# Pairs of edges spread over counting, ranking and scatter, and 12 instead of 16 of them beside every 16 state slots

## What is computed

```
xn = layernorm(x)                                   # no weights
proj = xn @ gat_w.T  (4 heads of 64);  s_src, s_tgt = per-head scores
e = leaky_relu(s_src[src] + s_tgt[tgt], 0.2);  exp_e = exp(e - max(e))
agg = segment_sum(proj[src] * exp_e, tgt) / segment_sum(exp_e, tgt)
h_local = layernorm(elu(agg + xn + gat_b))
deg = count of edges by src;  perm = argsort(deg + noise);  inv = argsort(perm)
y = mamba(xn[perm])      # conv of 4, then h = exp(dt*A) * h + dt*x*B, 16 states; y = h . C + D*x, gated
h_attn = layernorm(xn + y[inv]);  gate, feed-forward, layernorm;  x2 = x + that
out = x2 + sum of the 2 chosen of 8 experts of layernorm(x2)
```

## Time and profile before

| | |
|---|---|
| median of 3 runs | 4287.28 us (4280.2 to 4293.75) |
| profiled execution | 4285.63 us, span 4284.0 us, mean granted clock 0.839 |
| TensorE matmuls, weight loads | 3021.3 us (71%), 2270.9 us (53%) |
| VectorE | 3010.5 us (70%) |
| ScalarE | 1979.5 us (46%) |
| GpSimd | 2331.1 us (54%) |
| read from and written to memory | 389.97 MB and 63.43 MB |

### The profile page before, as it was taken

How to read it: one execution, slowest core, us unless ns; L and a number is a source line. 1 busy time by engine, 2 the same in 40 slices (tenths; PEclk the granted TensorE clock), 3 DMA queues, 4 the chain that set the end, 5 groups by cost and what they waited for, 6 DMA issues and landing times. The chain is left out here.

```text
span 4284.0 us, 66432 instructions
## 1 busy us (share of the span) xinstructions
PE 3021.3 (71%) x17205; PEld 2270.9 (53%) x17206; DVE 3010.5 (70%) x5576; ACT 1979.5 (46%) x4255; POOL 2331.1 (54%) x2215
## 2 busy tenths in 40 slices
PE   5333321177887888778887788787877488939998
PEld 4333311155655565556655565555655245528887
DVE  6677795478788878888788888888887488721111
ACT  2000000066666656666666666666665265613222
POOL 2000003557777777777777777777775357633443
PEclk8555555589998999999999999999998799969999
DMA  3100201334444444445444444444447433326665
GB/s 100 34 0 0 100 1 41 106 96 132 125 124 128 131 127 125 130 129 133 125 126 130 129 128 129 125 127 132 126 128 103 115 73 96 89 95 144 142 144 108
DMA packets 282877, 457.71 MB, mean 107 GB/s; under 512 B 56232, under 2 KB 202905, under 8 KB 282265
## 3 DMA queue, kind: packets, MB, share of 16 engines
q0 software_dynamic: 119472, 287.74, 28.4%
q1 hardware_dynamic: 163048, 165.86, 13.1%
HBM read 389.97 MB, written 63.43 MB: 106 GB/s over the span
## 5 line engine op out<-in xcount | busy, mean ns | idle before, releaser
L679 POOL DMA_INDIRECT el_g<-table,el_ix x1792 | 1796.5, 1003 | 689.7 <-issue 520.6
L1094 PE MATMUL fl_ps<-el_g,el_oh 128*128 128x260 f32 x3584 | 1029.4, 438 | 336.0 <-DVE ACC L802 333.0
L1094 PEld LDWEIGHTS fl_ps<-el_g,el_oh 128*128 128x128 f32 x3584 | 747.6, 215 | 707.5 <-issue 554.5
L822 DVE TENSOR_TENSOR_SCAN mb_h<-mb_dA,mb_h,mb_dB 128x224 f32<-128x224 f32 x896 | 573.9, 672 | 0.0
L792 DVE TENSOR_TENSOR el_g<-el_g,fl_pw 128x1024 f32<-128x1024 f32 x448 | 544.2, 1215 | 0.0
L953 ACT CAST el_oh<-fl_pt 128x512 f32<-128x512 bf16 x451 | 261.0, 579 | 425.0 <-PE fl_pt L1070 421.7
L1117 PE MATMUL fl_py<-mb_hc,ident 128*128 128x448 f32 x896 | 422.2, 553 | 0.1
L968 ACT ACTIVATE mb_dA<-mb_dt,mb_a 128x224 f32<-128x224 f32 x900 | 382.6, 475 | 2.9 <-DVE mb_dt L866 1.6
L811 DVE TENSOR_TENSOR mb_dB<-mb_u,fl_pbc 128x448 f32<-128x448 f32 x449 | 276.3, 615 | 135.4 <-PE fl_pbc L1107 134.5
L468 POOL DMA_INDIRECT sorted_x<-XN,rank x49 | 47.8, 975 | 588.8 <-DVEq L388 574.2
L939 ACT ACTIVATE el_away<-el_dst,el_less 128x512 bf16<-128x512 bf16 x452 | 325.3, 720 | 22.1 <-DVE mb_a L756 21.2
(11 more groups left out here) (300 smaller groups left out, 5405.8 us busy)
## 6 DMA issues: line engine op xcount, KB each, us to landing
el_dst<-dst_rows SPq DMA_DIRECT2D x452, 128.0 KB
el_g<-table,el_ix POOLq DMA_INDIRECT x1792
ex_w<-in_moe_W SPq DMA_DIRECT2D x56, 512.0 KB
ex_x<-routed_x SPq DMA_DIRECT2D x56, 257.0 KB, 2.8
mb_x<-sorted_x SPq DMA_DIRECT2D x30, 224.0 KB, 3.2
table<-px_tr POOLq DMA_DIRECT2D x49, 130.0 KB, 2.3
px_x<-in_x SPq DMA_DIRECT2D x49, 128.0 KB, 2.6
xn<-XN SPq DMA_DIRECT2D x1, 6272.0 KB
```

What stands on the lines that cost most here:

```text
L679: pool.indirect_dma_start(out=G[b // GU][:, b % GU * NJ + j, :], out_offset=None, in_=dram["table"], in_offset=bass.IndirectOffsetOnAxis(a ...
L822: nc.vector.tensor_tensor_scan(H[:, n % 2, k, :], dA[:, n % 4, k, :], dB[:, n % 2, k, :], H0[:, k, n % NS:n % NS + 1], ALU.mult, ALU.add). ...
L1094: mm = nc.tensor.matmul(pS, OH[:, n % (2 * GU), j, :], G[n // GU % 2][:, n % GU * NJ + j, :], start=j == 0, stop=j == NJ - 1)
```

## The change

`degrees`, `ranks` and `both_loops` become one stage, `streams`, of three blocks with barriers of all engines between them but no clearing of the edge semaphores. Pairs and state slots are numbered apart. There are 440 pairs.

1. `project`: no XN in SBUF. GpSimd's queue stores XS to `xn` in memory, tile by tile, ahead of the table rows of the same seven tiles; VectorE waits for that store before it writes XS again.
2. `pair_tables` comes straight after `project`.
3. Counting block, pairs 0 to 35. 34 steps of 46 edges instead of 46 of 34; the one-hots are laid out [value, edge], compared with REP, the values repeated 46 times, so that the innermost run of every operand is the 46 edges. TensorE reads weights and moving columns with a step of 46 elements.
4. Ranking block, pairs 36 to 91. Tiles are compared in the order 0, 48, 1, 47 and so on, one in each slot from the sixth on.
5. Third block. Pairs 92 to 95: after each one's gathers GpSimd issues 13 of the row scatters, from nine buffers that SyncE refills from `xn`. SyncE waits for all of them and loads the first block; pairs 96 to 103 go beside the preparing of block 0, two pieces each. Then 448 state slots, with pairs beside slots 0, 1 and 2 of every 4: 12 beside 16. GpSimd runs its own loop over 24 pairs in each turn, 5 ahead.

The inner functions of the edges and of the state (`logits`, `scale`, `add`, `one_hot`, `gather_sums`, `scan`, `prepare` and the others) are as before. Unchanged too: `nodes`, `plan`, `experts`.

```diff
-DB = 34
+DB = 46
+ND = DC // DB                      # 1564 // 46 = 34
+GB = 24
+G_COUNT, G_RANK, G_INTRO, G_LEAD = 36, 92, 104, 5
+PAIRS = G_INTRO + NC // 2 * GB      # 104 + 14 * 24 = 440
+def pair_beside(m):
+    at = m.n % 4
+    return Slot(m.i, G_INTRO + m.n // 4 * 3 + at, GB) if at < 3 else None
 # project, VectorE
-    nc.vector.tensor_scalar(at, X[:, j, :], ...)          # XN
     dve.wait_ge(turned, 1 + i * TG)
+    dve.wait_ge(kept_xn[j], 16 + i * 16)
     nc.vector.tensor_scalar(XS[:, j, :], X[:, j, :], ...)
 # project, GpSimd
+    for j in range(TG):
+        pool.wait_ge(scaled, 1 + i * TG + j + 1)
+        pool.dma_start(n_t[...], XS[:, j, :]).then_inc(kept_xn[j], 16)
+        def edges_vector(dve, S):
+            steps = logits(dve, S) if S.n % GU == 0 else None
...
+            add(dve, S - 3)
...
+            scale(dve, S - 1)
+        def edges_tensor(pe, S):
+            turn(pe, S + (GU - 1))
+            spread(pe, S + (GU - 1))
+            gather_sums(pe, S - 2)
 # counting block, VectorE
+    def mark_high(c):
+        if c >= 2:
+            dve.wait_ge(counted, c - 1)
+        nc.vector.tensor_tensor(HA[:, c % 2], HI[:, c * DB:(c + 1) * DB].unsqueeze(1).to_broadcast([P, SRC_HI, DB]),
+                                REP[:], ALU.is_equal).then_inc(split_hot, 1)
+    for q in range(G_COUNT):        # logits' first step before mark_high
+        mark_high(q); ...; add(dve, S - 3); ...; scale(dve, S - 1); mark_low(q)
 # counting block, TensorE
+    for q in range(G_COUNT):
+        edges_tensor(pe, pair(q))
+        c = q - 1
+        pe.wait_ge(split_hot, 2 * c + 2)
+        for e in range(DB):
+            mm = nc.tensor.matmul(count[:], HA[:, c % 2, :, e], HB[:, c % 2, :, e], ...)
+        mm.then_inc(counted, 1)
 # ranking block
+    tile_at = [t for u in range(NT // 2) for t in (u, NT - 1 - u)] + [NT // 2]
+    for q in range(G_COUNT, G_RANK):
+        edges_vector(dve, pair(q))
+        if first <= q < first + NT:
+            compare(q - first)
 # third block, GpSimd
+    for k in range(SCAT + PREP):    # 4 + 8
+        p = pair(G_RANK + G_LEAD + k)
+        free(pool, p)
+        gather(pool, p, srcT[:, p.number, :])
+        for t in range(k * each, min((k + 1) * each, NT)):
+            pool.wait_ge(xn_loaded[b], t // len(XN) * 16 + 16)
+            pool.indirect_dma_start(out=dram["sorted_x"], in_=XN[b], ...).then_inc(placed[b], 16)
 # third block, SyncE
+    for k in range(SCAT):
+        for t in range(ahead + k * each, min(ahead + (k + 1) * each, NT)):
+            bring(t)                # waits placed[b] of tile t - 9
+        rows(sp, pair(G_RANK + k + 4))
+    for b in range(len(XN)):
+        sp.wait_ge(placed[b], -(-(NT - b) // len(XN)) * 16)
+    load(0)
+    for k in range(SCAT, SCAT + PREP):
+        rows(sp, pair(G_RANK + k + 4))
 # the slot of the loop, VectorE (ScalarE, TensorE and SyncE alike)
-    def slot(S, last=False):
+    def slot(M, S):                 # S is pair_beside(M), None in every fourth slot
...
+        if S:
+            add(dve, S - 3)
...
+        if S:
+            scale(dve, S - 1)
         prepare(c + 1, 1 - b, at)
-        inflow(S + 1)
+        inflow(M + 1)
```

More of the change, by code:

```diff
@@ L154, in build @@
         stage(constants)
[L155 to L159, removed]
+        stage(project, a, dram)
         with nc.sbuf_tensor("ACC", [P, NT, ROW], F32) as ACC, nc.sbuf_tensor("emax", [P, NH], F32) as emax, \
@@ L201, in project @@
     passed = sem("passed")
+    kept_xn = [sem(f"xn_stored{j}") for j in range(TG)]
     wv, wv_sb, eps_set, kept = sem("score_weights"), sem("score_weights_sb"), sem("eps_set1"), sem("score_kept")
@@ L608, in both_loops @@
     brought = [sem(f"fl_dst{g}") for g in range(4)]
+    early = lambda v, least: isinstance(v, int) and v < least
     with ExitStack() as ctx:
@@ new lines, in free, with gather @@
+        def free(pool, p):
+            if not early(p.number, 2 * GU):
+                pool.wait_ge(s["summed"], p.number - 2 * GU + 1)
+                apart(pool, s["passed"])
+        def gather(pool, p, index):
+            b = p.n % (2 * GU)
+            for j in range(NJ):
+                pool.indirect_dma_start(
+                    out=G[b // GU][:, b % GU * NJ + j, :], out_offset=None, in_=dram["table"],
+                    in_offset=bass.IndirectOffsetOnAxis(ap=index[:, j:j + 1], axis=0)).then_inc(gathered[b], 16)
@@ new lines, in turn, with spread @@
+        def turn(pe, p):
+            q, n = p.number, p.n
+            pe.wait_ge(s["hot"], q + 1)
+            if not early(q, 1):
+                pe.wait_ge(s["turned_sb"], q)
+            for j in range(NJ):
+                mm = nc.tensor.transpose(pT[:, j, :], OHT[:, n % 2, j * P:(j + 1) * P], I16[:])
+            mm.then_inc(s["turned"], 1)
+        def spread(pe, p):
+            q, n = p.number, p.n
+            pe.wait_ge(s["hot"], q + 1)
+            if n % GU == 0 and not early(q, GU):
+                pe.wait_ge(s["logit"], p.of(GU) * 5)
+            k = pe.value_load(tile_of[0:1, bass.ds(q, 1)], min_val=0, max_val=NT - 1)
+            for j in range(NJ):
+                mm = nc.tensor.matmul(pX[:, n % GU * NJ + j, :], OHT[:, n % 2, j * P:(j + 1) * P],
+                                      parts[:, bass.ds(k, 1), :].rearrange("p o c -> p (o c)"),
+                                      start=True, stop=True, skip_group_check=True)
+            mm.then_inc(s["spread"], 1)
@@ new lines, in gather_sums @@
+        def gather_sums(pe, p):
+            q, n = p.number, p.n
+            pe.wait_ge(s["scaled"], q + 1)
+            pe.wait_ge(s["turned_sb"], q + 1)
+            if not early(q, 1):
+                pe.wait_ge(s["added"], q)
+            for j in range(NJ):
+                mm = nc.tensor.matmul(pS, OH[:, n % (2 * GU), j, :], G[n // GU % 2][:, n % GU * NJ + j, :],
+                                      start=j == 0, stop=j == NJ - 1)
+            mm.then_inc(s["summed"], 1)
+        def edges_vector(dve, S):
+            steps = logits(dve, S) if S.n % GU == 0 else None
+            if steps:
+                next(steps)
+                next(steps)
+                next(steps)
+            add(dve, S - 3)
+            if steps:
+                next(steps)
+                next(steps)
+            scale(dve, S - 1)
```

1332 lines of the change are left out of this document (686 added, 646 removed).

## The result

The changed kernel takes 4364.51 us (median; 4363.57 to 4365.64) against 4284.25 for the kernel before on the same chip: ratio 1.0184, 95% interval 1.0168 to 1.02. It is slower by 1.8%; I had forecast 4085. Its profiled execution took 4363.7 us, with a span of 4362.1.

The account below looks back on a forecast made before the run. GpSimd's queue was taken to bound the loop, full for 94% of the period, VectorE next. Span 4284.0 + 122 (front) - 323 (loop) = 4083, given as 4085 us; range 3985 to 4185.

Parts of the forecast that it names:

- 46 count matmuls are 4.1 at 1.2: Counting block, TensorE: the count matmuls of one slot take 4.1 us at 1.2 GHz, 2.05 if they scale with the clock.
- the ring: Counting slot: add, gather_sums, count matmuls, mark_high wait on each other in turn; 7.6 us at full clock, 11.3 at half, 8.9 taken.
- the phase: Counting block of 36 slots, 34 with marks at 8.9 us each: 339 us in all.
- The loop: State loop: a period of 16 slots falls from 87.45 to 75.9 us, giving 323 us less.
- the one for the B/C copies: State loop: VectorE's wait for copies that stand behind the convolution on TensorE stays at about 4.8 us a period.
- rival (c): State loop: TensorE takes over, the gather wait becomes one for TensorE; period 80, 113 us more, 4198; chance 10 in 100.
- Marks at 0.58 ns an element: Counting block, VectorE: with adjacent 16-bit elements mark_high takes 2.6 us and mark_low 1.7.
- rival (a): Counting block: marks stay at 1.09 ns an element, mark_high 4.9 us; 85 us more, 4170; chance 12 in 100.
- rival (b): Ranking block: comparisons hold GpSimd's gathers, 3.8 us for two slots, 93 in all, 4178; chance 8 in 100.
- Ranking: Ranking block: 49 slots with a comparison at 6.0 us, 7 at 5.2 and 3 for the barrier, 333 us.
- Rival (d): State loop: engine hand-overs keep slots without a pair at 3.67 us; period 85.7, kernel 4357, slower; chance 4 in 100.
- 122 us later: Everything ahead of the state loop: first state slot at 995 us instead of 873, from 176 + 339 + 333 + 147.

Follow-up runs that it names:

- the fastest kernel: Changed kernel with each mark value stored adjacently, the addition before mark_high and each mark written in two halves of 23 edges: 4048.8 us, ratio 0.9451 to the kernel before.

## Why the prediction was wrong

**The step that failed**: "46 count matmuls are 4.1 at 1.2 (89 ns each, 139.8 / 1564, where the granted clock was 0.50) and 2.05 if they scale". The 89 ns are those of a matmul whose operands lie adjacent. I had noted that the layout was turned and priced that for VectorE alone, which writes the marks; for TensorE, which reads them, I took the row of the old layout, and gave the link no upper bound. Measured: 8.44 us at either clock level. It enters the ring with 4.4 us over the value at half clock and 6.2 over that at full clock; it also keeps TensorE busy, and the granted clock was 0.56 there against 0.71 with adjacent reads, so gather_sums was 3.5 to 3.8 us in every slot, near its half-clock value. Ring 14.95 instead of 8.9, 34 x 6.05 = 206 of the 225 us by which the phase was missed; the kernels with adjacent reads give 194 back, directly.

**The other 19 us of that phase** lie all but one ahead of the first mark: 38 us from the start of the phase (178) to mark_high instead of 20. VectorE waited there 19.1 us for the first gathers, of which the first was held for 16.37 us. In the kernels without REP it is not held and the first mark comes 13.7 us sooner; what holds it stays open.

**Point by point.**
- Projection and pair tables: 178 for 176. The loop: 77.0 for 75.9, on VectorE's work of 64.9 us a period (1816.12 / 28), as said, but the idle time stands elsewhere. The wait for gathers is gone, as said; the one for the B/C copies, which I kept at 4.8, fell to 0.5 a period; in its place VectorE waits for the logits' inputs from TensorE. Two groups of the loop from 1500 to 3300 us, 23.4 periods:

```profile
L1020 DVE TENSOR_TENSOR mb_dB<-mb_u,fl_pbc 128x448 f32<-128x448 f32 x371 | 226.6, 611 | 12.8 <-PE fl_pbc L1258 12.0
...
L516 DVE TENSOR_REDUCE el_s<-fl_px 128x128 f32<-128x384 f32 x70 | 38.9, 555 | 193.8 <-PE fl_px L604 172.1 <-issue 21.8
```

- 172.1 / 23.4 = 7.4 us a period: the wait for TensorE of rival (c) did come. It took the place of other idle time, so the period is 1.1 us over the forecast and not the 4.1 at which (c) was priced. That the period came out near 75.9 is in part luck: the idle time was kept at 10.7 us for one reason and is 12.1 for another.
- Marks at 0.58 ns an element: 2504 and 1683 ns for 2.6 and 1.7, rival (a) refuted. The row that the 0.58 came from is an int32 shift with one input, so no row bore it out for two bf16 inputs. By the Trainium skill (VectorE: DVE Perf Modes, the perf-mode tier table), where a bf16 tensor_tensor in SBUF has twice the plain rate, mark_high is an estimated 2.5 us; the trace agrees.
- Comparisons hold no gather: beside them (780 to 1090 us) a gather takes 950 ns; rival (b) refuted. Marks hold them: 1670 ns in the mean with the ring opened. The Trainium skill (SBUF — State Buffer, SBUF: two separate sides) says that a VectorE operation takes the port pair that it shares with GpSimd if it runs in a two-port mode, or if it has two SBUF inputs and the GpSimd operation reads SBUF; both numbers agree with that.
- Ranking: 362 for 333, and about as much (361 to 367) in every kernel here that has the edge slots in it. Waits at the head of each group of four for TensorE (17.4 us of 310) and at the additions (15.5) are what the trace shows beyond my sum. No run was made of it.
- The ring itself: named and placed well and, with adjacent reads, sized well (7.11 and 9.37 measured, 7.6 and 8.9 said).
- Rival (d), the one on the slower side, came near the time (4357) by another way: its mechanism, a loop period of 85.7, did not occur. The loop gave back 298 us (first to last scan: 873.5 to 3327.7 before, 1252.2 to 3408.2 after). The loss was in the front, 379 us for the 122 said, where I had no rival for TensorE's price at all.
- The sum hid its best terms. The "122 us later" held some 130 us gained by quick marks and 63 by a wait that the new order no longer has (the prediction doesn't name it), against some 315 spent on moved slots. Written apart, the marks would have stood out as a gain by itself, and their layout as the thing on which it hangs.

**Still open**: what holds the first gather, the 29 us of ranking, why the loop of the fastest kernel is shorter than its siblings', and whether fewer than 36 slots beside the counting would be better still.

## What to carry to other kernels

When a layout is turned for the engine that writes a tile, price it for the engine that reads it as well; a duration row holds for its access pattern as much as for its shape. Where both engines want different innermost axes, look for a form that suits both: here each scalar stored twice side by side gave VectorE its pairs and TensorE its adjacent rows. And split a change into its independent gains before summing: some 130 us came from the marks, 63 from a wait that was longer than it had to be, and at most 43, on chips like the first, from the move that gave the change its name.

## What was unexpected of the hardware

- TensorE's reading of 16-bit operands with a step: free at 4 bytes (51 ns a matmul at 2.4 GHz, 49 when adjacent), 94 ns at 8, 169 to 185 ns from 16 to 92 bytes (7.79 to 8.53 us for 46), and 184 ns at 92 bytes both at 1.2 and at 2.4 GHz. One far-stepped operand is nearly as bad as two (157 ns with the moving one alone far-stepped, 179 with the weights alone).
- The slow matmuls count as busy time: TensorE is 81% busy from 216 to 742 us (426.0 of 526) at a granted clock of 0.56, and 65% busy at 0.71 with adjacent reads (204.25 of 313). Of those busy 426 us, 287 were count matmuls at less than half the pace that adjacent reads gave: the busy share alone did not tell this.
- VectorE wrote a bf16 comparison at 0.555 ns an element with innermost runs of only two elements.
- A first gather took 16.37 us in one set of kernels and 0.94 in the other, beside the same memset of VectorE.
